# Row-tiled gated heads, loads to spaced partitions, fp32r strips for the last attention, and bias and shared-expert work moved

## The chip, the cores and the metric

The kernel runs on one core of one Trainium2 chip. The metric is device microseconds (us) of one launch, lower is better. The engines are TensorE (PE; its weight loads are shown as PEld), VectorE (DVE), ScalarE (ACT), GpSimd (POOL) and SyncE (SP), which issues most DMAs. They run in parallel and meet at semaphores.

## The reference, cut to what matters

Two batches of 512 tokens with 128 channels go through two decoder layers. Layer 0: layernorm, a gated self-attention (16 heads of 8 channels, scores scaled by a sigmoid gate of the query), mixed with two 4-head attentions ("causal" and "meta"), a one-head cross attention over 77 keys, and a mixture of experts with GELU. Layer 1: layernorm, a self-attention whose inputs are quantised to 8 bits (16 heads of 8), a cross attention with 16 heads of 8 over the 77 keys, and a mixture of experts with SiLU and a shared expert.

```python
scores = einsum('bhqd,bhkd->bhqk', q, k) / sqrt(HD)      # 16 heads, HD = 8
mod    = sigmoid(hidden @ cg_W + cg_b + (cons_vec @ am_W + am_b))
probs  = softmax(scores * mod.transpose(0, 2, 1)[..., None], axis=-1)
ctx    = einsum('bhqk,bhkd->bhqd', probs, v)
```

## The kernel before, in words

**Stages in time.** Start and gated, causal and meta attention (to 305 us of the profiled span), wide cross attention (to 325), `experts_gelu` (to 476), `quantised_attention` (to 640), `cross_attention_heads` (to 738), `experts_silu` (to the end).

**One attention, in steps.** Class `Attention` runs jobs: a job is one group of heads (four gated, two wide) of one batch. `_schedule` writes one list of steps, and each engine walks the same list and does its part:

- A: two score products with queries in the output's rows; DVE takes the negated maximum over the keys (line 487). A job of four heads has 8 A blocks of 2 products (4 query tiles x 2 head pairs).
- M: the maxima are transposed by PE (L424), cast by ACT (L536), split by DVE (L494) and written by SP's DMAs (L560) as further rows of the query stack, so that the next product subtracts the maximum.
- B: the score product again, keys in the output's rows (L438), followed by Exp on ACT (L528). One B is a "unit": one head and one tile of 128 keys, so a job of four heads has 16.
- V: the product of probabilities and values, fp32, four heads in four column strips of 32 (L452). E copies it out (ACT, L542), T transposes it (L461) and DVE divides it.

The list starts with `lead_blocks` A blocks (12 in the gated and the quantised attention) before the first B. In the gated attention it also holds the projections of later heads (P on PE, Q for the second part and the loads), the mixes (C, D), in fixed places counted in units.

**Exactness.** To be as exact as fp32, a query and key are cut into three bf16 parts (or two fp32r parts), and the contraction holds the pairs of parts under each other: 6 pairs x 8 channels = 48 rows, padding to 72 and 2 rows for the maxima (72 rows in A, 74 in B). `sp_load` (L714) issues the loads of such a stack: 6 for a bf16 stack, each from 128 partitions to 8 adjacent partitions times 16 heads. Constant rows (zeros, ones) are spread by three DMAs on ACT's queue at the start.

**Quantised attention.** The bias of the projection enters by 4 fp32 products of one row and 512 columns (L1931) and 8 of 128 (L1935), at the stage's start, ahead of the products with the input. The heads lie in strips of 32 partitions (`StripJob`), bf16.

**Last cross attention.** `PairJob` and `CrossJob` keep two heads in 64-row sides (48 rows used). The queries are loaded by 24 DMAs of 64 KB (two sides x six places x two batches) to 8 partitions each, and a job's maxima by 4 DMAs.

**SiLU experts.** PE first computes the routing logits (L2226, 8 products), then the shared expert's up products for two half batches, waits for the routing on DVE, and goes on through 8 expert pairs.

## Time and profile before

| | us |
|---|---|
| median of 3 runs (797.33 to 806.68) | 806.39 |
| the profiled execution | 810.68 |
| its span, first to last instruction | 808.6 |
| PE / PEld / DVE / ACT / POOL busy | 646.1 / 341.5 / 405.2 / 377.1 / 93.6 |

The profile is one execution of the program. Busy times of engines overlap; what sets the time is read stage by stage, from gaps, from who waits for whom, and from TensorE's granted clock (1.0 is 2.4 GHz, 0.5 is 1.2 GHz), whose mean was 0.801. The difference of 2.1 us between the execution and its span lies around the program.

### The profile page before, as it was taken

How to read it: one execution, taken by the hardware profiler on the slowest of the kernel's cores; microseconds unless marked ns; L12 is line 12 of the kernel's file. 1: busy time of each engine (PE TensorE's matmuls, PEld its weight loads, DVE VectorE, ACT ScalarE, POOL GpSimd, SP SyncE). 2: the span in 40 equal slices, each digit the busy share in tenths (PEclk: the TensorE clock that was granted, in tenths of full speed). 3: DMA queues.
4: the chain of work that ended last, by engine and by line, in shares of the span. 5: the costliest groups of instructions: out<-in, count | busy, mean ns of one | idle time of the engine just before them, and what ended most of it. 6: DMA issues, size and time to landing. Idle time of an engine off the chain costs nothing. (4 is left out here: it accounts for less than half of the span.)

```text
span 808.6 us, 9225 instructions
## 1 busy us (share of the span) xinstructions
PE 646.1 (80%) x3255; PEld 341.5 (42%) x3255; DVE 405.2 (50%) x806; ACT 377.1 (47%) x655; POOL 93.6 (12%) x80
## 2 busy tenths in 40 slices
PE   4089859999996977699999965798888427986798
PEld 2013223333333334599999934112221312324686
DVE  3077546677713755712221346868870723414554
ACT  3026736676663234554444521368885124443321
POOL 4101200110001000700000001980000010002100
PEclk9558989999999577599999965559995655557799
DMA  8405240353005008000000000000000041000000
GB/s 212 83 1 79 29 51 1 50 68 42 3 1 78 2 9 352 0 1 2 13 1 1 1 0 1 0 2 1 2 2 1 0 58 22 2 1 1 0 1 27
DMA packets 15456, 24.28 MB, mean 30 GB/s; under 512 B 2779, under 2 KB 10507, under 8 KB 15027
## 3 DMA queue, kind: packets, MB, share of 16 engines
q1 hardware_dynamic: 14048, 21.77, 14.0%
q10 hardware_dynamic: 1363, 1.93, 1.0%
q8 instruction: 26, 0.43, 0.2%
q14 instruction: 19, 0.16, 0.1%
HBM read 9.99 MB, written 0.52 MB: 13 GB/s over the span
## 5 line engine op out<-in xcount | busy, mean ns | idle before, releaser
L487 DVE TENSOR_REDUCE negmax<-ps 128x2 f32<-128x1024 f32 x96 | 114.5, 1220 | 62.5 <-PE ps L417 62.2
L528 ACT ACTIVATE probs<-ps 128x512 f32<-128x512 f32 x192 | 106.2, 598 | 47.5 <-PE ps L438 45.6
L1604 PEld LDWEIGHTS ps<-wproj,hid 128*128 128x128 f32 x640 | 83.4, 192 | 6.7
L1604 PE MATMUL ps<-wproj,hid 128*128 128x128 f32 x640 | 84.1, 275 | 0.0
L528 ACT ACTIVATE probs_q<-ps,score_scale 128x512 f32<-128x512 f32 x128 | 77.3, 691 | 13.1 <-PE ps L438 12.7
L1654 ACT ACTIVATE hid<-ps 128x512 f32<-128x512 f32 x80 | 47.5, 597 | 66.9 <-PE ps L774 66.9
L774 PE MATMUL ps<-h,wfc 128*128 128x512 f32 x240 | 76.9, 432 | 0.0
L487 DVE TENSOR_REDUCE negmax_q<-ps 128x2 f32<-128x1024 f32 x64 | 73.8, 1209 | 5.6 <-PE ps L417 5.6
L417 PE MATMUL ps<-k_gated,q_gated 72*128 72x512 bf16 x128 | 45.4, 443 | 27.0 <-DMA k_gated<-parts 20.9
L438 PE MATMUL ps<-q_gated,k_gated 74*128 74x512 bf16 x128 | 47.1, 410 | 8.3 <-DMA q_gated<-q_gated 8.2
L1764 DVE SCALAR_TENSOR_TENSOR x_tok<-ps,comb,x_tok 128x128 f32<-128x128 f32 x64 | 18.0, 344 | 69.3 <-PE ps L1604 69.3
L417 PE MATMUL ps<-k_strips,q_strips 32*128 32x512 bf16 x128 | 34.9, 481 | 14.8 <-DVE negmax_q L487 5.9
L438 PE MATMUL ps<-q_strips,k_strips 32*128 32x512 bf16 x128 | 40.2, 467 | 7.8 <-ACT probs_q L528 6.7
L452 PE MATMUL ps<-probs_q,v_q 128*32 128x512 f32 x256 | 44.3, 776 | 0.0
L774 PEld LDWEIGHTS ps<-h,wfc 128*128 128x128 f32 x240 | 41.2, 198 | 4.1
L139 PE MATMUL ps<-ident,xn 128*128 128x128 f32 x48 | 13.8, 440 | 32.4 <-DVE xn L106 32.3
L503 DVE RECIPROCAL inv<-ps 128x16 f32<-128x16 f32 (+1 forms) x32 | 7.7, 240 | 64.0 <-PE ps L461 63.8
L774 PE MATMUL ps<-h_parts,up_parts 128*128 128x512 f32 x108 | 32.7, 444 | 4.2 <-DVE hid L2341 3.2
L452 PE MATMUL ps<-probs,v_gated 128*32 128x512 f32 x256 | 35.5, 628 | 0.0
L452 PE MATMUL ps<-probs,v_wide 128*64 128x512 f32 x128 | 34.5, 628 | 0.3
L417 PEld LDWEIGHTS ps<-k_gated,q_gated 72*128 72x128 bf16 x128 | 10.4, 104 | 54.9 <-issue 27.4
L417 PE MATMUL ps<-k_wide,q_wide 96*128 96x512 f32 x64 | 29.1, 549 | 5.4 <-issue 3.0
(355 smaller groups left out, 919.0 us busy)
## 6 DMA issues: line engine op xcount, KB each, us to landing
q_wide<-parts SPq DMA_DIRECT2D x12, 256.0 KB, 5.5
k_wide<-parts SPq DMA_DIRECT2D x12, 256.0 KB, 6.9
wfc<-in_L_ffn_Wfc_dram SPq DMA_DIRECT2D x1, 2560.0 KB, 9.3
wproj<-in_L_ffn_Wproj_dram SPq DMA_DIRECT2D x1, 2560.0 KB, 15.0
q_gated<-parts SPq DMA_DIRECT2D x12, 128.0 KB
k_gated<-parts SPq DMA_DIRECT2D x12, 128.0 KB
qs_x<-parts_x SPq DMA_DIRECT2D x24, 64.0 KB
w<-in_L_ffn_W_dram SPq DMA_DIRECT2D x1, 1024.0 KB, 17.0
```

Source lines behind the costliest of these rows:

```text
L139: nc.tensor.transpose(K.ps[:, self.banks[b], P * (i % TPB):P * (i % TPB) + P], K.xn[:, i, :], K.ident[:, :]).then_inc(self.turned, 1)
L417: last = nc.tensor.matmul(ps[:, bank, at:at + size], rows, keys, start=True, stop=True, skip_group_check=True)
L438: nc.tensor.matmul(ps[0:size, self.B_BANK + g % self.B_SLOTS, :], job.k_at(j, k0, size, 2), job.q_at(j, job.q0, S, 2), start=True, stop=Tr ...
L452: last = nc.tensor.matmul(ps[job.width * j:job.width * (j + 1), self.O_BANK, :], job.v[0:size, job.b, i, job.heads[j], :], self.probs[0:si ...
L487: nc.vector.tensor_reduce(maxima, scores, AX.X, ALU.max, negate=True).then_inc(self.a_max_done, 1)
L503: nc.vector.reciprocal(inv, tile[:, :, :, hd]).then_inc(self.sums_inverted, 1)
L528: nc.scalar.activation(self.probs[0:size, g % self.P_SLOTS, :], ps[0:size, self.B_BANK + g % self.B_SLOTS, :], ACT.Exp, scale=scale).then_ ...
L774: last = nc.tensor.matmul(out, weights(a), moving(b), start=(start and i == 0), stop=(stop and i == 2), skip_group_check=True)
L1604: last = nc.tensor.matmul(K.ps[:, y_bank(g), i * P:(i + 1) * P], hid[:, m % SLOTS, i * P:(i + 1) * P], wproj[:, FT * e + f, :], start=(f = ...
L1654: nc.scalar.activation(hid[:, m % SLOTS, :], K.ps[:, 2 + m % 4, :], ACT.Gelu).then_inc(n["gelu_done"], 1)
L1764: last = nc.vector.scalar_tensor_tensor(out=K.x_tok[:, t, :], in0=y[:, i, :], scalar=comb[:, t, e:e + 1], in1=K.x_tok[:, t, :], op0=ALU.mu ...
```

## The change

1. **Gated heads.** Two heads share the 128 partitions: each has a side of 64 rows (`PairJob`; 16 slots become 8). The six pairs of parts are written at every 8th partition (`stack[c::8]`: 16 partitions x 8 pairs of heads in one DMA), and the maxima go to rows 6 and 7 of each group of eight. The projection's weights are interleaved by column (`interleaved`), so that heads come out by side. The padding DMAs are gone: DVE fills the whole query stack with zeros, POOL the key stack with ones, and POOL fills rows 96 to 127 of the wide keys. An A block's two products now use the two 64-row halves of the array, and so do neighbouring B's.
2. **Start.** Keys are projected first, after half of the layernorm; three loads of each of the first two stacks are issued by SP, three by ACT (step L). The first job has two heads, and 8 A blocks stand ahead of the first B, growing to 12 over the next 16 units (`lead_growth = 4`).
3. **Quantised attention.** The 4 bias products of 512 columns stand at the end of `experts_gelu`; the 8 of 128 columns become 2 of 512. The same `lead_blocks`, growth and split first job; E moves from ACT to DVE.
4. **Last cross attention.** fp32r in two parts: strips of 32 rows, written at every 4th partition, 3 loads of 256 KB for each batch, one of them by ACT. A is one product of K=128 and 320 columns for a query tile (before: two of K=112 and 154 columns); B has K=32; the maxima of a job go by 2 DMAs.
5. **SiLU experts.** The shared expert's first two up products come ahead of the routing logits, two more before the routing weights are needed.

```diff
 class PairJob(Job):
-    ROWS, SIDE = 48, 64
-    max_dmas = 4
+    SIDE, STEP, PARTS = 64, 8, 6
     def q_at(self, j, t0, n, more):
         at, h = self.SIDE * (j % 2), self.heads[j]
-        return self.q[at:at + self.ROWS + more, h // 2, t0:t0 + n]
+        return self.q[at:at + self.SIDE, h // 2, t0:t0 + n]
...
-class CrossJob(PairJob):
+class CrossJob(Job):
+    stride = CTX_PAD                                    # 80
+    STEP, PARTS = 4, 3
+    def q_at(self, j, t0, n, more):
+        return self.q[32 * j:32 * j + 32, self.heads[0] // 4, t0:t0 + n]
     def products(self, heads, q0):
-        both, first = self.SIDE + self.ROWS, self.heads[0] // 2
-        return [(2 * c * self.keys, 2 * self.keys, self.q[0:both, first + c, q0:q0 + P],
-                 self.k[0:both, first + c, :, self.k0:self.k0 + self.keys]) for c in range(self.G // 2)]
+        g = self.heads[0] // 4
+        return [(0, self.G * CTX_PAD, self.q[:, g, q0:q0 + P], self.k[:, g, :, self.k0:self.k0 + CTX_PAD])]
...
                 wanted = min(len(blocks), (self.held_lead if first else self.lead_blocks)
-                             + 2 * (n // 4) + self.A_PLACES[n % 4])
+                             + 2 * (n // 4) + self.A_PLACES[n % 4] + min(n // 4, self.lead_growth))
...
+            elif kind == "E" and self.evacuate_on_vector:
+                nc.vector.tensor_copy(self.osb[0:rows, u % 2, :], ps[0:rows, self.O_BANK, :])
...
+        if it.get("step"):
+            pairs = PAIRS if it["parts"] == 3 else PASSES
+            places = [(pair[it["kind"] == "k"], it["stack"][c::it["step"], :, it["s0"]:it["s0"] + it["cols"]])
+                      for c, pair in enumerate(pairs)]
...
+def interleaved(nc, out, w, moving, sides):
+    size = P // sides
+    for s in range(sides):
+        last = nc.tensor.matmul(out[s * size:(s + 1) * size], w[:, s::sides], moving, start=True, stop=True,
+                                skip_group_check=True)
+    return last
...
-    q16 = sb("q_gated", [P, 16, T], BF16, st)
-    k16 = sb("k_gated", [P, 16, T], BF16, st)
+    q16 = sb("q_gated", [P, 8, T], BF16, st)
+    k16 = sb("k_gated", [P, 8, T], BF16, st)
...
-            act.wait_ge(filled_pool, 3)
-            act.dma_start(q16[48:72, :, :], zeros.unsqueeze(1).broadcast_to([24, 16, T])).then_inc(padded, 16)
-            act.dma_start(k16[48:74, :, :], ones.unsqueeze(1).broadcast_to([26, 16, T])).then_inc(padded, 16)
-            act.dma_start(wide_k[96:98, :, :], wide_ones.unsqueeze(1).broadcast_to([2, 4, T])) \
-                .then_inc(padded, 16)
...
+            fill_stack(nc.gpsimd, k16[:, :, :], 1).then_inc(made_k, 1)
...
+            nc.gpsimd.memset(wide_k[96:128, :, :], 1.0).then_inc(made_wide, 1)
...
+            fill_stack(nc.vector, q16[:, :, :], 0).then_inc(made_q, 1)
...
+            pe.wait_ge(n["gelu_done"], M)
+            pe.wait_ge(n["constants"], 11)
+            Q.bias_first(K)
             next_ln.turn(pe, 1)
...
+            eng.dma_start(as_f32(X.q[c::4, :, half(b)]), as_f32((q_high, q_low)[part][:, half(b)])) \
+                .then_inc(s["stacked"][b], 16)
...
             for m in range(M + LAG):
-                if m < M:
+                if m == SHARED:
+                    raw()
+                if m < AHEAD:
                     up(m)
-                if m == SHARED:
+                if m == AHEAD - 1:
                     pe.wait_ge(n["made"], 4)
                     pe.wait_ge(n["comb_ready"], 1)
```

How the steps stand on PE at the program's start (names are out<-in; `negmax` is step M, `q_gated,k_gated` with the query named first is a B, with the keys first an A). Before:

```order
L139 MATMUL ps<-ident,xn 128x128 x8
L1203 MATMUL ps<-modulation 128x1
L634 MATMUL ps<-h_ft,square_weights 128x512 x3
L631 MATMUL ps<-square_weights,h_ft 128x128 x4
L417 MATMUL ps<-k_gated,q_gated 128x512 x18
L424 MATMUL ps<-ident,negmax 4x128 x4
L417 MATMUL ps<-k_gated,q_gated 128x512 x6
L438 MATMUL ps<-q_gated,k_gated 128x512
L417 MATMUL ps<-k_gated,q_gated 128x512 x2
```

Of the change:

```order
L796 MATMUL ps<-modulation 64x1 x2
L796 MATMUL ps<-bias_columns,ident 64x19 x2
L796 MATMUL ps<-bias_columns,ident 32x19 x4
L140 MATMUL ps<-ident,xn 128x128 x8
L796 MATMUL ps<-h_ft,square_weights 64x512 x6
L659 MATMUL ps<-square_weights,h_ft 128x128 x4
L438 MATMUL ps<-k_gated,q_gated 128x512 x10
L445 MATMUL ps<-ident,negmax 2x128 x4
L438 MATMUL ps<-k_gated,q_gated 128x512 x6
L459 MATMUL ps<-q_gated,k_gated 128x512
L438 MATMUL ps<-k_gated,q_gated 128x512 x2
```

The first transposition of maxima stands behind 10 A products instead of 18, and the first B behind 16 instead of 24.

On PE where `experts_gelu` ends and `quantised_attention` begins. Before:

```order
L1604 MATMUL ps<-wproj,hid 128x128 x12
L139 MATMUL ps<-ident,xn 128x128 x4
L1574 UNCONDITIONAL_BRANCH
L1927 UNCONDITIONAL_BRANCH
L1931 MATMUL ps<-ones_row,qkv_bias 128x512 x4
L1935 MATMUL ps<-qkv_bias,ones_row 128x128 x8
L1941 MATMUL ps<-xq,wq_high 128x512
```

Of the change:

```order
L1671 MATMUL ps<-wproj,hid 128x128 x12
L1500 MATMUL ps<-ones_row,qkv_bias 128x512 x4
L140 MATMUL ps<-ident,xn 128x128 x4
L1641 UNCONDITIONAL_BRANCH
L2005 UNCONDITIONAL_BRANCH
L2008 MATMUL ps<-qkv_bias,ones_row 128x512 x2
L2015 MATMUL ps<-xq,wq_high 128x512
```

The four wide bias products moved ahead of the last transposition of the layernorm, into the stage before.

SP's DMAs from the quantised to the last cross attention (`mparts` are maxima, L560 or L588). Before:

```order
L560 DMA q_strips<-mparts_q 4x512 x16
L1926 UNCONDITIONAL_BRANCH
L2109 UNCONDITIONAL_BRANCH
L732 DMA qs_x<-parts_x0 8x8x512 x12
L732 DMA qs_x<-parts_x1 8x8x512 x12
L560 DMA qs_x<-mparts_x 1x2x512 x32
```

Of the change:

```order
L588 DMA q_strips<-mparts_q 4x512 x14
L2004 UNCONDITIONAL_BRANCH
L2194 UNCONDITIONAL_BRANCH
L2194 DMA qs_x<-q_high_x 32x4x512
L2194 DMA qs_x<-q_low_x 32x4x512
L2194 DMA qs_x<-q_high_x 32x4x512 x2
L2194 DMA qs_x<-q_low_x 32x4x512
L588 DMA qs_x<-mparts_x 4x512 x16
```

SP issues 5 loads of queries instead of 24 (a sixth is ACT's), and half as many of maxima.

## Rows read from the trace of the kernel before

**Rows 1.** The core's line, and the page's clock row in 40 slices of 20.2 us.

```profile
core 0: 808.6 us, clock 0.801
PEclk9558989999999577599999965559995655557799
```

**Rows 2.** Busy time by stretch, then PEclk, DMA share, GB/s: two load times.

```profile
24.00:38.00 14.00, 0.00 (x0) 0.00 (x0) 0.00 (x0) 0.00 (x0) 1.08 (x1) 0.50 0.55 82
156.00:165.00 9.00, 8.24 (x48) 3.74 (x50) 6.02 (x12) 6.26 (x12) 1.27 (x1) 1.00 1.08 131
```

**Rows 3.** Timeline of the start: start us, us, engine, line, instruction, idle before.

```profile
3.89 3.52 POOL L753 MEMSET v_gated<- 128x4096 f32 x1
10.99 0.58 ACT L128 COPY h_ft<-ps 128x512 f32<-128x512 f32 x1 [2.06 <-PE ps L139]
23.03 5.20 SPq L732 DMA_DIRECT2D k_gated<-parts  x6
23.93 1.15 POOL L709 TENSOR_TENSOR parts<-rest,parts 128x512 bf16<-128x512 f32 x1 [0.79 <-ACT parts L667]
40.35 1.87 PE L417 MATMUL ps<-k_gated,q_gated 72*128 72x512 bf16 x4 [20.89 <-DMA k_gated<-parts]
55.79 0.61 PE L438 MATMUL ps<-q_gated,k_gated 74*128 74x512 bf16 x1
```

**Rows 4.** Timeline: the maxima of the fourth gated job and the B behind them.

```profile
104.33 1.29 SPq L560 DMA_DIRECT2D q_gated<-q_gated  x2
118.29 0.61 PE L438 MATMUL ps<-q_gated,k_gated 74*128 74x512 bf16 x1 [8.15 <-DMA q_gated<-q_gated]
```

**Rows 5.** Busy by stretch (PE PEld DVE ACT POOL, PEclk, DMA): gated and quantised attention.

```profile
56.00:135.00 79.00, 66.54 (x310) 23.63 (x308) 46.20 (x53) 47.81 (x85) 7.16 (x6) 0.85 0.31 41
152.00:217.00 65.00, 61.37 (x334) 23.64 (x332) 46.53 (x56) 45.47 (x84) 5.07 (x4) 1.00 0.37 50
560.00:600.00 40.00, 34.31 (x251) 9.18 (x244) 35.89 (x39) 36.51 (x64) 0.00 (x0) 1.00 0.01 2
118.00:124.00 6.00, 5.71 (x18) 2.11 (x18) 2.45 (x2) 2.41 (x5) 0.00 (x0) 0.50 0.00 0
```

**Rows 6.** Timeline: two A products on one array, 72 rows, and strips of 32.

```profile
49.75 1.03 PE L417 MATMUL ps<-k_gated,q_gated 72*128 72x512 bf16 x2 [0.18 <-DVE negmax L487]
506.24 0.61 PE L417 MATMUL ps<-k_strips,q_strips 32*128 32x512 bf16 x2 [0.53 <-DVE negmax_q L487]
```

**Rows 7.** The reductions of line 487: duration ns min/median/max, first and last start us.

```profile
L487 DVE TENSOR_REDUCE negmax<-ps x96: 1210/1224/1226, 41.4 to 273.9; 128x2 f32<-128x1024 f32 x96
```

**Rows 8.** Timeline around the start of the quantised attention.

```profile
472.20 1.15 PE L139 MATMUL ps<-ident,xn 128*128 128x128 f32 x4 [3.55 <-DVE xn L106]
477.56 7.16 PE L1931 MATMUL ps<-ones_row,qkv_bias 1*128 1x512 f32 x8 [4.21 <-PEq L57]
484.52 3.62 PE L1935 MATMUL ps<-qkv_bias,ones_row 1*128 1x128 f32 x16
503.18 1.03 PE L417 MATMUL ps<-k_strips,q_strips 32*128 32x512 bf16 x4 [3.83 <-DVE q_strips L1923]
515.54 1.18 SPq L560 DMA_DIRECT2D q_strips<-mparts_q  x2
517.89 0.60 PE L438 MATMUL ps<-q_strips,k_strips 32*128 32x512 bf16 x1 [0.59 <-DMA q_strips<-mparts_q]
```

**Rows 9.** Timeline: the last cross attention's loads, first A and first B.

```profile
649.70 15.70 SPq L732 DMA_DIRECT2D qs_x<-parts_x  x24
663.81 1.21 PE L417 MATMUL ps<-ks_x,qs_x 112*128 112x154 bf16 x8 [13.79 <-DMA qs_x<-parts_x]
675.53 0.64 PE L438 MATMUL ps<-qs_x,ks_x 50*77 50x512 bf16 x1 [4.62 <-DMA qs_x<-mparts_x]
```

**Rows 10.** Timeline: SiLU experts, the routing weights ready and the next up product.

```profile
758.47 0.29 DVE L2363 TENSOR_TENSOR comb_parts<-comb_rest,comb_parts 128x128 bf16<-128x128 f32 x1
763.84 1.65 PE L774 MATMUL ps<-h_parts,up_parts 128*128 128x512 f32 x6 [0.93 <-ACT comb_t L2297]
```

More of the change, by code:

```diff
@@ L712, in threes, with loads, load @@
         return self.number(n, lambda x: x["kind"] in "qk" and x["parts"] == 3)
-    def sp_load(self, sp, n):
+    def loads(self, n):
+        it = self.items[n]
+        if it.get("step"):
+            pairs = PAIRS if it["parts"] == 3 else PASSES
+            places = [(pair[it["kind"] == "k"], it["stack"][c::it["step"], :, it["s0"]:it["s0"] + it["cols"]])
+                      for c, pair in enumerate(pairs)]
+            return sorted(places, key=lambda x: x[0])
+        places, row, hd, count = [], 0, it["hd"], it["parts"]
+        for size in range(count, 0, -1):
+            for part in range(size):
+                at = row + hd * (part if it["kind"] == "q" else size - 1 - part)
+                places.append((part, it["stack"][at:at + hd, :, it["s0"]:it["s0"] + it["cols"]]))
+            row += size * hd
+        return sorted(places, key=lambda x: x[0])
+    def load(self, eng, n, first=0, end=None):
         it = self.items[n]
@@ L1454, in __init__ @@
         self.v = sb("v_x", [P, NB, 1, 16, 32])
         self.full = sb("full_kx", [P, keys])
-        self.rest = sb("rest_kx", [P, keys])
-        self.parts = sb("parts_kx", [P, 3, keys], BF16)
-        self.n = {x: K.sem("kx_" + x) for x in ("made", "projected", "full", "first", "rest", "second", "third", "v_out",
-                                                "stacked")}
-        self.item = dict(kind="k", stack=self.k, hd=8, parts=3, s0=0, cols=keys, pair=True)
-    MADE = 6
+        self.parts = sb("parts_kx", [P, 2, keys], F32R)
@@ L1464, in constants, with bias @@
+        self.n = {x: K.sem("kx_" + x) for x in ("made", "projected", "full", "first", "second", "v_out", "stacked")}
+    def bias(self, name):
+        at = COLUMNS.index(name)
+        return self.K.by_strip[:, at:at + 1]
+    MADE = 8
     def constants(self, pool):
         ops, chain = self.K.nc.gpsimd, Chain(pool, self.n["made"])
-        chain(ops.memset(self.k[:, :, :, :].rearrange("p c s t -> p (c s t)").bitcast(F32), 0.0))
-        chain(ops.memset(self.k[32:64, :, 0, :], 1.0))
-        chain(ops.memset(self.k[96:128, :, 1, :], 1.0))
+        keys = as_f32(self.k[:, :, :, :])
+        chain(ops.memset(keys.rearrange("p g j t -> p (g j t)"), 0.0))
+        for j in range(4):
+            chain(ops.memset(keys[32 * j:32 * j + 32, :, j, :], 1.0))
@@ L1514, in load @@
         n, loads = self.n, 0
-        sp.wait_ge(n["made"], 3)
-        for part in range(3):
-            sp.wait_ge((n["first"], n["second"], n["third"])[part], 1)
-            row = 0
-            for size in range(3, 0, -1):
-                if part < size:
-                    for dst, rows in stack_places(self.item, row + 8 * (size - 1 - part)):
-                        sp.dma_start(dst, self.parts[rows, part, :]).then_inc(n["stacked"], 16)
-                        loads += 1
-                row += size * 8
+        sp.wait_ge(n["made"], 5)
+        for c, (_, part) in enumerate(PASSES):
+            sp.wait_ge(n[("first", "second")[part]], 1)
+            for j in range(4):
+                for b in range(NB):
+                    sp.dma_start(as_f32(self.k[32 * j + c:32 * j + 32:4, :, j, b * CTX_PAD:b * CTX_PAD + CTX_LEN]),
+                                 as_f32(self.parts[32 * j:32 * j + 32, part, b * CTX_LEN:(b + 1) * CTX_LEN])) \
+                        .then_inc(n["stacked"], 16)
+                    loads += 1
         sp.wait_ge(n["stacked"], 16 * loads)
@@ L2134, in _ @@
             ln.vector(dve)
-            stks[0].split(dve, nc.vector)
+            for b in range(NB):
+                low_part(dve, b)
             att.vector(dve)
@@ L2364, in _ @@
                                     ALU.subtract).then_inc(n["comb_ready"], 1)
-            for m in range(SHARED):
-                product(m)
             cut_low(dve, 2)
```

377 lines of the change are left out of this document (219 added, 158 removed).

## The prediction

> **What bounds the kernel now.** I read the clock first: TensorE was granted 0.801 on average, 0.5 from 20 to 60 us, high in both gated stages, low again in the last cross attention [rows 1]. Then the timeline of the start. The first score product begins at 40.35 after a wait of 20.89 us for the loads of the key stack, the first B at 55.79, and in between PE does 24 A products at half clock while each A block waits for DVE [rows 3]. So 40 us pass before anything repeats, half of it for DMAs; those run at a DMA share of only 0.55 and 82 GB/s, where loads of the wide stacks to more partitions reach 1.08 and 131 GB/s [rows 2].
>
> Then busy times by stretch [rows 5]. In the gated stage of batch 0 (79 us for 64 units) and batch 1 (65 us, again 64) DVE has 46.2 and 46.5 us of work and ACT 47.8 and 45.5, but PE 66.5 and 61.4: PE is the bound there. Batch 0 holds one stall as well, 8.15 us for the maxima of the fourth job: SP issues them at 104.33, and B starts at 118.29 [rows 4]; they lie in the queue behind stack loads. In the quantised stage, the same work with heads in strips of 32 rows, DVE and ACT are busy for 35.9 and 36.5 of 40 us and PE is not the bound. Why PE is slower in the gated stage is in the timeline: two A products of 72 rows take 1.03 us one behind the other, while two of 32 rows, side by side in the array, take 0.61 [rows 6], both while the clock was 0.5. The reductions take 1.22 us each in both stages [rows 7].
>
> **The change part by part.** The sum is made against the profiled execution's own 810.7 us; the median of the runs shown, 806.4, is 4.3 below.
>
> 1. *Start, first A.* The new loads go to 16 partitions instead of 8, and the padding DMAs are gone (24 and 26 rows x 16 heads x 1024 tokens x 2 bytes: 1.6 MB). No row shows such a destination. From below: they gain nothing and stay at 82 GB/s (131 KB in 1.6 us, six in 9.6 us). From above: 131 GB/s or better (1.0 us each). I take the upper, as the copied size is that of the wide loads' class and the padding no longer competes. The chain that feeds them is earlier too: the projections need only half of the layernorm, ready on ACT at 10.99 + 0.58 = 11.6 [rows 3], but POOL, which makes the parts, first fills stacks (3.52 us for 4096 words, rows 3; three such fills, some 12 us) and is free at about 15. Before, POOL's last part ended at 25.1 and A started 15.3 behind. Now the last parts are there at about 21, SP and ACT issue in parallel, and six loads at 1.0 us land by 27: first A at **27, −13.4**. At 82 GB/s it would be 31. DVE's fill of the query stack at the very start costs about 3.5 us, hidden under the loads of x but for 0.5.
>
> 2. *Fill, first A to first B.* 15.4 us for 24 products and a round trip of maxima. Now 16 products stand ahead of B, and the maxima start behind 10. Eight products fewer are four blocks of 1.22 us [rows 7] = 4.9, of which 0.5 is lost to the round trip showing: **−4.4**.
>
> 3. *Gated, batch 0.* If pairs of products on two 64-row halves overlap as strips do [rows 6], PE's work falls by 0.4 us in each A block and about as much for B pairs, to about 45 us, and DVE and ACT become the bound. The batch costs the busier one's time over the share that it reaches in the quantised stage (36.5 of 40, so 0.90): DVE 46.2 plus the four postponed blocks 4.9 = 51.1, over 0.90 = 57. The clock stays low for the first part, as it was from 40 to 66; there PE needs up to 0.3 us more a unit for some 24 units: +7. 79 − 64.5 = **−14.5**. The stall of 8.15 lies in the 79, and its cause (a queue of slow loads) goes with part 1.
>
> 4. *Gated, batch 1.* 46.5/0.90 = 52: **−13**. The two causal stages start with fewer leftovers: −1.5.
>
> 5. *Quantised attention.* The bias products take 7.16 and 3.62 us at half clock [rows 8]. The first four move ahead of the layernorm's last transposition, where PE stood idle for 3.55 us [rows 8]; at full clock they take 3.6 and fit. If they don't hide, they cost up to 3.6 there. The 8 small ones (3.62) become 2 wide ones (half of 7.16): nothing. So −7.2. The fill from first A (503.18) to first B (517.89) shrinks like part 2, −4.2, of which DVE gives back 2.5 later where it is near its limit. A split first job has another M, E and T: +1. E moves from ACT, 0.6 us a job, to DVE: between −3 and +3, taken 0. Sum **−7.9**.
>
> 6. *GELU experts.* POOL's fills and the key loads of the last attention lie in a stage of 150 us in which POOL has little to do: 0. If they slow SP's weight loads, +2.
>
> 7. *Last cross attention.* SP's 24 loads of 64 KB take 15.70 us and PE waits 13.79 for them [rows 9]; now there are six of 256 KB to 32 spaced partitions, of which ACT issues one. At 131 GB/s [rows 2] six take 12 us but they start as each half is ready; the first batch's three, 6 us, release the first job: first A at 655.5 instead of 663.8, **−8.3**. The fill to the first B (11.7 us, B waits 4.62 for maxima) loses two of four DMAs a job, −2.5. In the steady part B strips overlap but fp32r A products of 320 columns cost more: −3 (from 0 to −6). Sum **−13.8**.
>
> 8. *SiLU.* The routing, which ended at 758.47, starts two up products later, and one more is done by then (six take 1.65 or 2.93 us): +0.5, from −1 to +4 [rows 10].
>
> Sum: −13.4 −4.4 −14.5 −13 −1.5 −7.9 −13.8 +0.5 = −68.0, so 743 for a profiled execution and 739 unprofiled; I say 740.
>
> On the loads, by the Trainium skill ("SBUF — State Buffer", section "Door 1: The DMA port swizzle") eight adjacent partitions reach two of the 16 ports, 16 partitions spaced by 8 reach eight, and 32 spaced by 4 all sixteen. By that rule the cross attention's loads would be twice as fast as I took, and its first A 3 us earlier; the low share of rows 2 agrees with it, and no row shows a spaced destination.
>
> **The rivals.**
>
> *Pairs don't overlap.* Only strips of 32 have been seen side by side. If 64-row halves run one behind the other, gated PE time stays at 61 a batch: batch 1 gains nothing and batch 0 only its stall and part of the fill, so 20 of the 27.5 go: 763. For it: no row shows two 64-row halves at work. Against: rows 6. Chance 0.15.
>
> *Low clock persists.* PE's busy share falls in the gated stage, and the clock was 0.5 in stretches where PE waits a lot (20 to 60, and 650 to 730, rows 1), as well as in 118 to 124, where PE was busy for 5.71 of 6 us [rows 5]. At half clock a unit costs 1.2 us (five Exps in 6 us) instead of 0.9. For half of the 128 units: +20, 763. Chance 0.12.
>
> *Loads stay slow.* First A at 31 or later, the stall of rows 4 comes back (8), the cross attention's 8 are lost: 4 + 8 + 8 + 8 for further waits: about 769. Chance 0.08.
>
> *Upside.* The last cross attention is all at half clock [rows 1]. If denser work brings it to full clock it is 15 to 20 us shorter: 722. Chance 0.08.
>
> *Slower than before.* B of 64-row halves and V in column strips alternate at each unit, with M and T as whole-array products between. If each change of split lets the array drain for about a product's time, 0.61 [rows 6], 130 changes cost 78 and the 27.5 of parts 3 and 4 are lost: 848. It makes the kernel 2% slower from (826.6 − 743 − 27.5)/130 = 0.43 us a change. Against it: the quantised stage alternates in the same way, 40 us for some 54 units. Chance 0.03.
>
> The Trainium skill ("TensorEngine Tiling (Array Packing)", section "Key Properties") says that changing the tiling mode, not just the tile, drains the engine; by it the gated stages would lose something at each change; what it costs with strips is small enough for DVE and ACT to reach their share in [rows 5].
>
> **How the numbers follow.** The forecast, 740, has 0.54; its own range is ±13 from the ends above (start 4, clock term 7, quantised 4, cross 6, SiLU 3, most not together). The others: 0.15 at 763, 0.12 at 763, 0.08 at 769, 0.08 at 722, 0.03 at 848. From 716 to 768 leaves out the drain, half of the slow loads and the forecast's tails: 2 in 10. 2% is about what a measurement of this kernel tells from no change: 790 to 823. Below lie all but the drain and mixtures of two or three bad cases: faster 0.93, same 0.04, slower 0.03.
>
> **What would show it.** Start: the first score product near 27, with a DMA share near 1 from 18 to 27. Gated: pairs of A products in 0.6 us at low clock, DVE and ACT at 0.9 of the stretch, no idle for maxima at the fourth job; 64 units in 57 to 65 and in 52 us. Quantised: no row of one-row products behind the layernorm but two; first B 10 to 11 us after the first A. Cross: the first A within 15 us of the stage's start, a wait for maxima under 3. Wrong would make it a mean clock below 0.75, a pair that takes 1.0 us, or a new wait of DVE, which holds E in the quantised stage, seen in B's releasers as the maxima's split.

## The result, and the profile after

The changed kernel took 775.81 us (median of 4 runs, 767.06 to 776.76); its ratio to the kernel before, run beside it, is 0.963 with a 95% interval of 0.951 to 0.975. A second series gave 771.07 us and 0.955 (0.951 to 0.960). It is faster, by 31 us in the first series where 66 were forecast (806.4 to 740). The profiled execution has a span of 775.0 us (808.6 before).

```profile
core 0: 775.0 us, clock 0.830
PEclk9669999999995756799999966689995655557899
```

The line above and the page's clock row (40 slices of 19.4 us) answer to [rows 1]: the start's low stretch is shorter, the gated stages run at a mean clock of 0.93 (42 to 112, low only at its start) and 1.00 (129 to 194), and the last cross attention (629 to 697) is at half clock as before.

The start, from the timeline (start us, us, engine, line, instruction, idle before):

```profile
9.28 1.78 DVE L104 RECIPROCAL std<-std 128x4 f32<-128x4 f32 x1
11.11 4.25 DVE L107 TENSOR_SCALAR xn<-x_tok,mv,std 128x128 f32<-128x128 f32 x4
11.45 3.51 POOL L1251 MEMSET k_wide<- 32x4096 f32 x1
15.92 5.36 PE L796 MATMUL ps<-h_ft,square_weights 128*64 128x512 f32 x12
19.37 1.95 SPq L774 DMA_DIRECT2D k_gated<-parts  x3
31.67 1.04 PE L438 MATMUL ps<-k_gated,q_gated 64*128 64x512 bf16 x4 [9.30 <-DMA q_gated<-parts]
41.70 0.61 PE L459 MATMUL ps<-q_gated,k_gated 64*128 64x512 bf16 x1 [0.49 <-DMA q_gated<-mparts_gated]
```

The first A comes at 31.67 (40.35 before, [rows 3]), the first B at 41.70 (55.79). The first projection starts at 15.92, although half of the input was normalised at 11.1; DVE's second half takes 4.25 us beside POOL's fill of the wide keys.

Busy time by stretch (PE, PEld, DVE, ACT, POOL, then clock, DMA share, GB/s), the 64 units of batch 0 and of batch 1 of the gated attention; the third row is the loads' wait at the start:

```profile
42.30:112.10 69.80, 63.11 (x331) 17.64 (x328) 50.70 (x60) 48.12 (x87) 7.16 (x6) 0.93 0.25 47
129.40:194.20 64.80, 59.90 (x332) 19.33 (x333) 46.06 (x55) 45.11 (x83) 5.10 (x4) 1.00 0.38 50
27.00:31.60 4.60, 0.00 (x0) 0.00 (x0) 0.00 (x0) 0.00 (x0) 0.66 (x1) 0.50 0.64 171
```

Batch 0 takes 69.8 us (78.5 before) and batch 1 64.8 (65.0 before). In batch 1 DVE and ACT have the work of [rows 5] (46.1 and 45.1 us; DVE is busy for 0.71 of the time), and PE is nearly as busy as before (59.9, 61.4 before), though two A products in a pair now take 0.39 us and did take 0.60 at this clock. The new loads move 171 GB/s, against 82 in [rows 2].

Where the time went, from the starts of the first and last instruction of each part in the two timelines (us):

| part | before | after | moved | forecast |
|---|---|---|---|---|
| to the first A | 40.4 | 31.7 | -8.7 | -13.4 |
| first A to first B | 15.4 | 10.0 | -5.4 | -4.4 |
| gated batch 0, 64 units | 78.4 | 69.7 | -8.7 | -14.5 |
| gated batch 1, 64 units | 65.0 | 64.8 | -0.2 | -13 |
| the causal attentions | 39.8 | 40.3 | +0.5 | -1.5 |
| meta attention to GELU's last down products | 226.2 | 228.5 | +2.3 | 0 |
| quantised attention, from there to its last eight units | 151.5 | 146.8 | -4.7 | -7.9 |
| to the last cross attention's 24th unit | 95.2 | 83.6 | -11.6 | -13.8 |
| SiLU, with the end of the cross attention | 96.1 | 98.9 | +2.8 | +0.5 |

To see inside the gated stages, the starts of ACT's Exp instructions were taken every four units (a cycle: four B, two A, one V):

```
cycles of batch 1, us      8 with projections and mixes                2 with A of their own    6 with A of the causal heads
before                     5.0 5.4 3.8 4.3 3.6 5.4 4.0 4.0 (35.5)      3.0 4.4 (7.4)            3.1 4.1 3.3 4.4 3.1 4.1 (22.1)
after                      4.6 5.4 3.8 4.3 3.5 5.4 4.2 4.0 (35.2)      2.6 4.1 (6.7)            3.3 4.2 3.5 4.5 3.3 4.2 (23.0)
```

Only the two cycles in the middle behave as forecast. Two such cycles of after, on PE and DVE; first with A of the gated heads' own, then with the causal heads' (K of 96 rows, fp32r, the whole array):

```profile
163.27 1.06 PE L473 MATMUL ps<-probs,v_gated 128*32 128x512 f32 x8
164.27 0.39 PE L459 MATMUL ps<-q_gated,k_gated 64*128 64x512 bf16 x1
164.28 0.59 PE L438 MATMUL ps<-k_gated,q_gated 64*128 64x512 bf16 x2
164.50 0.58 PE L459 MATMUL ps<-q_gated,k_gated 64*128 64x512 bf16 x2
165.66 1.06 PE L473 MATMUL ps<-probs,v_gated 128*32 128x512 f32 x8
...
173.19 1.07 PE L473 MATMUL ps<-probs,v_gated 128*32 128x512 f32 x8
174.19 0.39 PE L459 MATMUL ps<-q_gated,k_gated 64*128 64x512 bf16 x1
174.50 0.73 PE L438 MATMUL ps<-k_wide,q_wide 96*128 96x512 f32 x2
175.17 0.39 PE L459 MATMUL ps<-q_gated,k_gated 64*128 64x512 bf16 x2
175.49 0.73 PE L438 MATMUL ps<-k_wide,q_wide 96*128 96x512 f32 x2
176.15 0.39 PE L459 MATMUL ps<-q_gated,k_gated 64*128 64x512 bf16 x1
176.47 1.07 PE L473 MATMUL ps<-probs,v_gated 128*32 128x512 f32 x8
```

From V to V the first takes 2.39 us (two reductions of 1.2 on DVE, which is never idle there), the second 3.28, PE without a gap. In the first, A starts 0.01 us after B, since one of its two products lies on the other half; in the second, every step from a half to the whole array or back shows 0.31 to 0.32 us from a single product's start to the next start.

### The profile page after: what moved, and what is told of

It reads as the page before. It is cut to its first block and busy times, and to the rows that moved or that the text cites. A ratio compares the mean times of both kernels' runs of the same rounds, so it can differ in the third digit from the quotient of the medians.

```text
span 775.0 us, 9266 instructions
## 1 busy us (share of the span) xinstructions
PE 638.4 (82%) x3271; PEld 329.1 (42%) x3271; DVE 419.2 (54%) x824; ACT 374.7 (48%) x649; POOL 97.2 (13%) x78
## 3 DMA queue, kind: packets, MB, share of 16 engines
q1 hardware_dynamic: 12436, 20.78, 11.7%
## 5 line engine op out<-in xcount | busy, mean ns | idle before, releaser
L473 PE MATMUL ps<-probs_q,v_q 128*32 128x512 f32 x256 | 46.8, 730 | 0.0
L438 PE MATMUL ps<-k_gated,q_gated 64*128 64x512 bf16 x128 | 29.8, 427 | 20.1 <-DMA q_gated<-parts 9.3
L459 PE MATMUL ps<-q_strips,k_strips 32*128 32x512 bf16 x128 | 38.5, 438 | 5.7 <-ACT probs_q L556 4.0
L438 PE MATMUL ps<-k_strips,q_strips 32*128 32x512 bf16 x128 | 31.6, 442 | 12.4 <-DVE negmax_q L509 4.4
L459 PE MATMUL ps<-q_gated,k_gated 64*128 64x512 bf16 x128 | 39.5, 394 | 1.3 <-ACT probs L556 0.8
L473 PE MATMUL ps<-probs,v_gated 128*32 128x512 f32 x256 | 39.1, 612 | 0.0
L731 POOL TENSOR_TENSOR parts<-full,parts 128x512 fp32r<-128x512 f32 x8 | 10.2, 1272 | 159.5 <-ACT parts L688 159.5
L438 PE MATMUL ps<-k_wide,q_wide 96*128 96x512 f32 x64 | 26.4, 505 | 4.5 <-issue 2.8
```

The costliest lines, as they stand in the source:

```text
L438: last = nc.tensor.matmul(ps[:, bank, at:at + size], rows, keys, start=True, stop=True, skip_group_check=True)
L459: nc.tensor.matmul(ps[0:size, self.B_BANK + g % self.B_SLOTS, :], job.k_at(j, k0, size, 2), job.q_at(j, job.q0, S, 2), start=True, stop=Tr ...
L473: last = nc.tensor.matmul(ps[job.width * j:job.width * (j + 1), self.O_BANK, :], job.v[0:size, job.b, i, job.heads[j], :], self.probs[0:si ...
L731: ops.tensor_tensor(self._part(n, 1), full, as_f32(self._part(n, 0)), ALU.subtract) \
```

## Experiments

Each is the changed kernel with one edit, unless said otherwise. Times of stages are from each run's own profile, so that they don't depend on how the kernel before fared beside it (its medians were 798 to 809 in the four series). "Batch 1" is its 64 gated units; they take 64.8 us in all eight profiles whose edits leave its cycles alone, so that 0.7 us there is clear.

The quantised stage, counted from its first Exp to that of the last cross attention, took 149 us in both profiles of the changed kernel and 142 to 150 in variants that leave it as it is. The long ones spent more of it at a clock of 0.5: 64 us of 149.3 in the changed kernel (with four dips of 3.4 us and more between 500 and 568), 43 of 142.3 in the variant that changes only the last stage. So totals of 768 to 776 are told apart only by their stages.

### What a change of the array's split costs

A kernel of its own: x is copied, and TensorE does series of products on zeros, with no waits.

```diff
+cycle(b, a): b(0); a(); b(1); b(2); a(); b(3); v()     # v: four fp32 products in four column strips
+cycle(b, a), grouped: b(0); b(1); a(); a(); b(2); b(3); v()
```

> This kernel computes nothing of the reference: it only copies x and lets TensorE do series of products of 512 columns on zeros, with no wait between them: whole-array bf16; 64-row halves in turn; one half alone; whole and half in turn; and ten cycles each of the order B A B B A B V (V: four fp32 products in four column strips) with B of 74 rows or of 64-row halves, A of two 96-row fp32r products or of two bf16 products. Drain theory (a change of the array's split costs about 0.1 us, read from 0.32 us between starts after a change against 0.21 without): whole and half in turn 0.31 us a product at full clock against 0.21; the cycle with fp32r A takes 2.95 us with 74-row B and 3.2 to 3.3 with 64-row B; the cycle with bf16 A takes 2.7 with 72 and 74 rows and 2.3 to 2.4 with halves. No-drain theory: whole and half in turn 0.21; the cycle with fp32r A gets 0.2 us shorter with halves, 2.75. Grouped order B B A A B B V: drain theory 2.9 or less with fp32r A, no-drain theory 2.5.

Measured, timeline of PE at full clock:

```profile
27.57 7.07 PE L79 MATMUL ps<-mov_whole 128*128 128x512 bf16 x31
34.57 3.63 PE L79 MATMUL ps<-mov_halves 64*128 64x512 bf16 x32
38.04 7.07 PE L79 MATMUL ps<-mov_one_half 64*128 64x512 bf16 x32
45.36 10.00 PE L79 MATMUL ps<-mov_mixed 64*128 64x512 bf16 x31 [0.26 <-issue]
```

Per product, of 32 each: whole array 0.22 us, halves in turn 0.11, one half alone 0.22, whole and half in turn 0.31. So a change costs 0.09. What in the array takes that time isn't told apart. The cycles, V to V, each the same within 0.02 us in ten repeats:

| cycle | B of 74 rows (before) | B of 64-row halves (after) | grouped, halves |
|---|---|---|---|
| A of two fp32r products, 96 rows | 2.92 | 3.28 | 2.77 |
| A of the gated heads' own | 2.84 | 1.97 | 1.97 |

The drain theory holds for the first row (2.95 and 3.2 to 3.3 were expected). The kernel's own cycle with wide A stands exactly at 3.28, so PE bounds it. In this series the change makes it 0.36 us longer; in the kernel the six cycles with wide A went from 22.1 to 23.0, 0.15 each, as they weren't at PE's 2.92 before. For the second row the theory's sizes were off (2.7, and 2.3 to 2.4, were expected), but the row says why the own cycles gain: PE's 2.84 fell under DVE's 2.44.

### What the overlap is worth in place

```diff
+            self.a_blocks = [([qt], [[j], [j + 2]]) for j in range(2) for qt in range(TPB)]
+            self.units = [(kt, j) for kt in range(TPB) for j in (0, 1, 3, 2)]
```

> Only the order of heads within a gated job is changed: an A block's two products, and neighbouring B's, lie on the same 64-row side, so they can't overlap, while loads, splits and everything else stay. If overlap is worth what the rows show (a pair takes 0.39 instead of 0.60 at full clock, 0.61 instead of 1.03 at half), and PE is what binds: batch 1's 64 units, 64.8 us now, take 20 A blocks and 16 B pairs x 0.21 = 7.6 us more, 72; batch 0's 69.7 us about 8 to 12 more; total about +16 us, 792. If the chain of waits (DVE, ACT's evacuation of projections) binds: less than +4 us in each batch, total under +8.

Measured 777.3 us (the profiled execution 770.84); batch 0 70.6, batch 1 66.6 (+1.8), causal attention of batch 0 +1.7. The edit takes away only part of the overlap. Within an A block and between two neighbouring B's it is gone, but a B and the A next to it now often lie on different sides and start together:

```profile
167.00 0.39 PE L466 MATMUL ps<-q_gated,k_gated 64*128 64x512 bf16 x1
167.00 0.60 PE L445 MATMUL ps<-k_gated,q_gated 64*128 64x512 bf16 x2
```

In batch 1 two such products start within 0.1 us of each other 36 times in the changed kernel and 15 times here. The 21 lost overlaps are worth 4.4 us at 0.21 each; PE's busy time rose by 3.6 us (59.9 to 63.5), and the batch by 1.8. So the view that PE alone binds falls, since half of what PE lost did not show. What batch 1 would take without any overlap, no run says. That gain and cost are a draw is read from the cycles themselves: -0.7 in the two with A of their own, +0.9 in the six with wide A, -0.3 in the eight with projections and mixes.

### Another order of A and B

```diff
 class GatedAttention(Attention):
+    A_PLACES = (0, 0, 2, 2)
```

> Only the places of A in the gated attention's list are changed: B B A A B B V instead of B A B B A B V, so a cycle of four units has two B pairs instead of one and two changes of split fewer where A is a wide whole-array product. Drain theory: where A is wide (some 24 units of each batch) 3.28 us a cycle becomes about 2.9; where A is gated, B pairs save up to 0.21 a cycle; with 0 to 0.3 of waiting for DVE at the second A; the two batches together 3 to 6 us shorter, total about 771. Waits theory: two A's in a row find no free slot, DVE is starved between, and each cycle gets longer by 0.3 to 1.0 us: total +5 to +15.

Measured 800.73 us, batch 1 80.2. PE alone needs less in this order (2.77), but the stage is 1 us a cycle slower, so the waits theory holds for it. Timeline, last column the wait:

```profile
206.63 0.60 PE L445 MATMUL ps<-ident,negmax 128*2 128x128 f32 x4 [1.67 <-DVE negmax L509]
209.88 0.61 PE L459 MATMUL ps<-q_gated,k_gated 64*128 64x512 bf16 x2
210.42 1.73 PE L438 MATMUL ps<-k_wide,q_wide 96*128 96x512 f32 x4
211.68 1.23 DVE L509 TENSOR_REDUCE negmax<-ps 128x2 f32<-128x1024 f32 x1 [2.63 <-PE ps L438]
```

PE waits 1.67 us for the maxima of the group it has just done, and while it does M, T and V, DVE has nothing to reduce for 2.63.

The same in the last cross attention alone, where PE is never idle:

```diff
+class CrossAttention(Attention):
+    A_PLACES = (0, 0, 2, 2)
```

> Only in the last cross attention A goes to the order B B A A B B. There PE is never idle in the steady part (7.43 us a job at half clock), DVE needs 0.8 us an A, so a second B pair that overlaps saves 0.64 us for each of eight jobs: 39.3 us from the first Exp to the 25th becomes 36 to 36.8, total -4 to -5 us. Rival, from the grouped gated list that got 1 us a cycle slower: the second A waits for DVE, 0.3 us or more a job comes on top and the gain is under 2 us.

Measured 775.14 us; the stretch of 24 units went from 39.3 to 40.9 us. PE now waits for DVE at M and for the Exp behind it; the rival holds here too.

### What binds the cycles with a projection

```diff
-            last = interleaved(nc, K.ps[:, bank, 0:it["cols"]], it["w"], ...)
+            cols = it["cols"] if n < 4 else 64
+            last = interleaved(nc, K.ps[:, bank, 0:cols], it["w"], ...)
```

> Left out: seven eighths of the columns of every query, key and gate projection inside the gated attention's list (64 columns instead of 512 are computed; ACT, DVE, POOL and the loads do all their work, on old data). PE then needs 0.9 us less for each of them: 3 of batch 1's gated part in the list's first half of batch 0, and 4 in batch 1. If PE's own time for projections is what keeps batch 1 at 1.01 us a unit: 64.8 becomes about 61. If ACT's two reads of 0.68 us (the wait of 0.8 us of A for them) bind instead: 63.5 to 65.

Batch 1 62.9 us: -1.9 of the 3.6 that PE was spared. Neither of the two.

```diff
-        nc.scalar.activation(full, product, ACT.Identity, bias=it["bias"])
+        c = cols if n < 4 else 64
+        nc.scalar.activation(full[:, 0:c], product[:, 0:c], ACT.Identity, bias=it["bias"])
```

> Left out: seven eighths of ACT's first read of each wide projection's result inside the gated attention's list (`full`, 64 columns instead of 512; the rest of it is old data), 0.45 us of the 1.37 that ACT needs before A gets the slot. PE, DVE, POOL and loads do all their work. If the chain PE projection, ACT's reads, A, DVE's reduction sets the cycles with a projection: 0.3 to 0.45 us less for each of the four in batch 1's gated part, its 64.8 us becomes 63.0 to 63.6. If these cycles are bound by the sum of PE's work: no change, 64.6 to 64.9.

Batch 1 64.1 us: -0.7, of 1.8 spared on ACT. Both edits together:

> Left out: seven eighths of the columns of PE's projections inside the gated attention's list and of ACT's first read of them, as in the two kernels that left out one of them. One chain: the savings add up or more, batch 1's gated part 62.2 us or less (64.8 - 1.9 - 0.7), 61 if what the first removes lets the second show in full. Two things side by side, of which each hides the other: 62.5 to 63.

61.8 us, -3.0. Each of the three is one execution. The savings add up, and in the same cycles (the second, sixth and seventh get 0.4 to 0.5 us shorter by the first edit, 0.2 to 0.4 by the second, 0.7 to 0.8 by both), as one chain would have it: P holds one of the two slots for PE's 1.1 us and ACT's 1.4, and A and DVE have the other. Of the 5.4 us spared, 2.4 still don't show. The waits of after in batch 1 (PE, what it waited for: us, times, longest) name the same step:

```profile
PE ps L438 <- ACT parts L688: 2.4, 3, 0.8
PE ps L438 <- DVE v_wide L705: 0.8, 2, 0.4
```

A direct try, a bank of its own for everything but A, taken from B:

```diff
 class GatedAttention(Attention):
+    B_SLOTS, OWN_BANK = 2, 6
```

> In the gated attention the results of projections, transpositions and mixes (P, M, T, C, D) get a PSUM bank of their own instead of one of the two slots that A blocks use; in return B has two banks instead of three. Everything else stays. Slot theory (in cycles of four units with a projection, A waits since a slot is held for 1.1 us by PE and 1.4 us by ACT's two reads, so DVE is served by one slot): those cycles, 4.6 to 5.4 us, fall by 0.5 to 1.0 us each, batch 1's 64.8 us becomes 57 to 61, both batches together about 10 us less. Sum-of-work theory (in these cycles PE or ACT simply have too much to do): no cycle falls by over 0.2 us. Should two B banks be too few, PE shows waits on ACT at B and the cycles without projection, 2.6 to 3.5 us, get longer; that would be seen apart.

Measured 783.8 us, batch 1 69.5: PE waits 5.8 us on ACT's Exp at B (8 times, longest 1.1). Two banks for B are too few, and the cycles with a projection got longer, not shorter. What a slot more would bring stays open; no bank is left to try it with.

### Lead, and E on DVE

```diff
-        super().__init__(K, "att0", jobs, lead, 8, ...)                       # lead_growth = 4
+        super().__init__(K, "att0", jobs, lead, 12, ...)                      # lead_growth = 0
-    att = QuantAttention(K, "attq", jobs, 2, 8, ...)
+    att = Attention(K, "attq", jobs, 2, 12, ...)                              # first job of four heads
```

> The gated and the quantised list start with 12 A blocks and don't grow, as in the kernel before, and the quantised attention's first job has four heads again; all else stays. Theory that the shorter lead is only a loan: gated, first B 4 to 5 us later (46.5 instead of 41.7) and batch 0's 64 units 4 to 5 us shorter (65), so the causal attention starts at the same time within 1 us; quantised, first B 4.7 us later after the first A, the first 32 units 4 us shorter, the stage the same within 1 us. Theory that it gains in full: the first B later by 4.7 and no unit faster, total +8 to +9 us.

Measured 774.31 us (768.39 in the profiled execution, the fastest of five). Gated: the first Exp comes at 46.7 instead of 42.3, and the 64th is over at 112.1 in both. The shorter lead is a loan, paid back in full within batch 0. Quantised: the first Exp comes 3.0 us later, and the stage takes 137.8 us after it, where the shortest variants with the short lead take 142.2 to 142.3: 1.5 in favour of the long lead, in profiles whose clock isn't the same (49 us at 0.5 against 43), so this one is less sure. The split first job went out with the short lead, and no run parts the two.

```diff
-    att = QuantAttention(K, "attq", jobs, 2, 8, ..., evacuate_on_vector=True)
+    att = QuantAttention(K, "attq", jobs, 2, 8, ...)
```

> Only step E of the quantised attention (0.67 us for each job) goes back from DVE to ACT. DVE theory (DVE binds at full clock, two reductions of 1.22 in a cycle of 2.5): each of the nine jobs' cycle with E and T gets 0.3 to 0.6 us shorter, the stage about 3 to 5 us, total 771 to 773. Rival, ACT binds (four Exp of 0.61 to 0.69 in the same 2.5): the stage gets 0 to 4 us longer.

Measured 769.08 us. Four cycles (a job) with E on DVE take 2.5 4.6 2.6 2.5 (12.2), with E on ACT 2.8 3.8 2.6 2.5 (11.7), as before. So DVE binds, and moving E to it costs 0.5 us a job, 4 us in all by that. The whole stage is 142.3 us, as short as that of a variant with E on DVE that had 10 us less at the clock of 0.5, so its length alone doesn't show it. The combination further on does: with a lead of 12 its first 120 units take 89.3 us with E on ACT, where the variant above, with E on DVE, takes 93.5 (10 and 15 us of them at 0.5).

### The two ends of the program

```diff
-                if m == SHARED:
-                    raw()
+            raw()                                          # the whole stage as before
```

> Only the last stage goes back to the order of before: routing logits first, then the shared expert. If the new order costs what the two profiles say (96.1 us from the last attention's end to the end of the program before, 98.9 after, the wait of 4.9 us for the routing weights among it), this gets 2.8 us shorter; if the 2.8 comes from the clock there, no change.

Measured 767.78 us (767.73 to 769.47); from the last attention's 24th unit to the end 96.4 us instead of 98.9. The new order costs 2.5. Its wait, in the changed kernel, answers to [rows 10]:

```profile
728.13 1.04 PE L2366 MATMUL ps<-ident_bf,comb_parts 128*72 128x128 bf16 x8 [4.86 <-DVE comb_parts L2468]
```

```diff
-            ln.tensor(pe)
+            ln.turn(pe, 0)                      # and in P of the values: ln.turn(pe, 1) ahead of it
-            for b in range(NB):
-                ln.normalise(dve, b)
-            dve.wait_ge(gate_ready, 3)
+            ln.normalise(dve, 0)
+            dve.wait_ge(gate_ready, 3)          # then the gate's bias, then ln.normalise(dve, 1)
```

> At the start PE transposes only the first half of the normalised input ahead of the projections of batch 0, and the second half behind the query's projection; DVE sums the gate's bias ahead of normalising the second half. In the changed kernel the first projection starts at 15.92 since PE and DVE do the second half first, whose normalisation takes 4.25 us while POOL fills the wide keys (1.11 in the kernel before). If the projection's start is what sets the first A: first projection at 12.3, first A at 28 instead of 31.7, total -3.5. If POOL (busy with fills to 14.96) or the loads set it: first A not before 30.5.

Measured 769.63 us, first Exp at 37.1. Timeline:

```profile
10.44 1.31 DVE L107 TENSOR_SCALAR xn<-x_tok,mv,std 128x128 f32<-128x128 f32 x4
11.19 4.80 PE L796 MATMUL ps<-h_ft,square_weights 128*64 128x512 f32 x12 [0.67 <-ACT h_ft L129]
26.41 1.03 PE L438 MATMUL ps<-k_gated,q_gated 64*128 64x512 bf16 x4 [8.93 <-DMA q_gated<-parts]
```

The first projection starts 4.7 us earlier, and the first A comes at 26.41, 5.3 earlier and where the prediction had it (27). The projection's start was the missing step.

### A kernel that beats both, and the changed one again

The early projection, the last stage's order of before, E on ACT and a lead of 12 in the quantised attention, all in one:

> The changed kernel with what the runs found: early projection at the start (-5.2 us to the first Exp), the quantised attention with E on ACT (-0.5 us a job), 12 A blocks of lead and a four-head first job (first Exp 3 to 4.7 us later, 4.5 us less after it), and the last stage in the order of before (-2.5). Sum against the changed kernel: -5.2 - 4 - 0.5 - 2.5, about -12; if the quantised stage gets its full clock as in the variants so far (767 to 769 us where the changed kernel shows 767 or 776), 755 to 760; if these gains only shift the clock, 764 or more.

> The changed kernel itself once more. If the 7 us by which its profiled quantised stage is longer than that of variants which don't touch it come from the clock of an execution: its times fall into two groups, about 767 to 769 and 775 to 777, and no variant needs a gain of its own for 768. If they are its own work: all times at 775 or more.

Measured side by side: 758.13 us (755.21 to 760.70), ratio to the kernel before 0.940 (0.935 to 0.944), and the changed kernel 771.07 (768.62 to 774.55), ratio 0.955 (0.951 to 0.960). The combination is 13 us faster than the changed kernel, of which the quantised stage has the most: 131.6 us from its first Exp where the changed kernel shows 149, though its longer lead makes that first Exp some 4 us later. The changed kernel's times (five of six between 770.75 and 774.55) lie between the two groups that were expected, so they don't sort into two; its profile again has 149.1 us in that stage and the dips of the clock, which the combination's lacks. Why the clock dips in one and not in the other stays open: two variants that differ from the changed kernel only in a later stage (the grouped cross attention and the last stage's old order) don't dip.

## Why the prediction was wrong, step by step

**Gated batch 1, -13 forecast, -0.2 measured: this is the step that failed.** The prediction took the whole batch at the quantised stage's busy share, DVE's 46.5 us over 0.90, since both have "the same work". Measured, DVE is busy for 46.1 us of 64.8, a share of 0.71. The two stages don't have the same work. In the quantised list there are only A, B, V and their rounds; in batch 1 eight of sixteen cycles carry projections and mixes, and six carry the A blocks of the causal heads. Both could be read before: the fixed places of P, Q, C and D in the list, and a lead of 12 blocks, that is 24 units. Three sizes were wrong in it:

- The saving of a pair was read at half clock (1.03 to 0.61, [rows 6]) and applied to a stage at full clock, where it is 0.60 to 0.39. It was half as large.
- The changes of split were priced as a rival only, at a whole product's 0.6 us, and dismissed, as the quantised stage alternates freely. It does so among 32-row products and column strips only for V; in the gated stage each A of the causal heads takes the whole array between two B's. The price is 0.09 us in the plain series, and 0.36 in a cycle of the series after the overlap's gain is taken off, of which 0.15 shows in the kernel. The rival's mechanism is there; its threshold of 0.43 us a change is not reached. The rule of the Trainium skill that it named ("TensorEngine Tiling (Array Packing)", "Key Properties") agrees with the series of whole and half in turn (0.31 us a product against 0.22).
- In the cycles with a projection, much of what PE is spared turns into waiting for the slot: 3.0 us come back when the projections and ACT's reads are cut short. Batch 1 is then still 10 us above the forecast's 52. As an estimate, at the quantised stage's 12.2 us for four cycles the eight with projections and mixes would take 24.4 instead of 35.2, and the six with wide A some 18 instead of 23.0. So the excess lies in the two kinds that the quantised list doesn't have; beyond the 3.0 its cause stays open.

No rival fits. "Loads stay slow" is nearest in time (769), and had the first A "at 31 or later", where it came (31.67), by luck: the loads were fast and began late. "Pairs don't overlap" (763) has batch 1 unchanged, as it was, and is false in its mechanism: they do overlap. Its premise, that only strips of 32 had been seen side by side, was false too. The kernel before had it in its last cross attention, two B's of 50 rows at rows 0 and 64 in the time of one:

```profile
687.69 0.65 PE L438 MATMUL ps<-qs_x,ks_x 50*77 50x512 bf16 x2
```

**Gated batch 0, -14.5 forecast, -8.7 measured.** The stall of [rows 4] went, as forecast: its cycle takes 4.2 us instead of 12.3, and that is 8.1 of the 8.7. Against it stands the loan of the short lead (4.3), so some 4.9 us are left. They are not the overlap's: with the lead of before (the variant above), batch 0 takes 65.4 us, 13.0 less than before, and beside the 8.1 of the stall 4.7 of these lie in four cycles during which the kernel before ran in part at a clock of 0.5 (56 to 66, 87 to 90, 114 to 124). The changed kernel was at 0.5 only up to 52. The forecast had kept 7 us for the low clock (its 57 and 7 make 64, not 64.5). That the clock makes these 4.7 is read from the coincidence and not isolated; the other cycles are the same draw as in batch 1.

**Start, -13.4 forecast, -8.7 measured.** The loads were right: 171 GB/s, better than the 131 taken as a bound (at a DMA share of 0.64, where near 1 was to show it). The last parts were ready at 27.7 instead of 21. The forecast had the projections follow half of the layernorm; in the code PE transposes all eight tiles first, and DVE's second half was held up by POOL's fills, which had been costed at nothing for DVE. The early projection gives the missing 5 us. **The fill, -4.4**, was -5.4.

**Quantised attention, -7.9 forecast, -4.7 measured.** Up to the first A the gain was 6.2 of the 7.2: the four bias products did not hide wholly, they take 4.48 us and the layernorm's last transposition starts 7.2 us after GELU's last products instead of 6.4. The fill gave 4.7. Behind the first Exp, 120 units took 105.0 us instead of 98.7: E on DVE, taken as 0 between -3 and +3, costs 4, and the short lead is paid back there too, 4.5 by the variant with the long one, of which the forecast had 2.5. That makes more than the 6.3; the clock, at 0.5 for 30 us of these and for 41 before, may hide the difference.

```profile
448.43 4.48 PE L1500 MATMUL ps<-ones_row,qkv_bias 1*128 1x512 f32 x8
458.16 3.75 PE L2008 MATMUL ps<-qkv_bias,ones_row 1*128 1x512 f32 x4 [4.20 <-PEq L58]
476.83 1.03 PE L438 MATMUL ps<-k_strips,q_strips 32*128 32x512 bf16 x4 [3.82 <-DVE q_strips L2001]
486.82 0.60 PE L459 MATMUL ps<-q_strips,k_strips 32*128 32x512 bf16 x1 [0.40 <-DMA q_strips<-mparts_q]
```

These answer to [rows 8].

**Last cross attention, -13.8 forecast, -11.6 measured.** The loads and the fill brought more than forecast: PE waits 3.02 us where it waited 13.79 ([rows 9]), and the time to the first Exp fell by 14.7 in all. The prediction took 131 GB/s for these loads and thought twice as much possible; the six moved 360 (625.7 to 630.0). The steady part, forecast at -3, is +3.0 for 24 units: a job takes 7.43 us instead of 6.84.

```profile
628.53 1.31 PE L438 MATMUL ps<-ks_x,qs_x 128*128 128x320 f32 x4 [3.02 <-DMA qs_x<-q_low_x]
656.16 0.90 PE L438 MATMUL ps<-ks_x,qs_x 128*128 128x320 f32 x2
657.00 0.71 PE L459 MATMUL ps<-qs_x,ks_x 32*77 32x512 f32 x2
```

An A block of 320 columns takes 0.84 us to the next start where it took 0.62, two per job, and each B 0.06 more; the B pair overlapped before too. Its overlap had been counted as new.

**SiLU, +0.5 forecast, +2.8 measured,** 2.5 of it the new order. **Between, 0 forecast, +2.3:** the wide cross attention ran at a mean clock of 0.58 in 22 us (281 to 303) where it was 0.72 before (303 to 325); that this makes the 2.3 is not shown.

## What to carry to other kernels

A stage that is bound by one engine in one stretch is bound by others a few microseconds on: cut it into cycles, sort these by what they carry, and cost each kind, before a share from another stage is laid over the whole. Read a pair's saving at the clock of the stage that it is meant for, and count the products of another shape that lie between. Of three work moves in this change (E, the expert's order, the short lead) one was a loan and two cost time, while the gain lay in loads and in a stall that went.

## What the runs showed of the hardware

- Two products on the two 64-row halves take 0.11 us each in a series, where one half alone takes 0.22, as the whole array does; a change between the whole array and a half adds 0.09 us, at full clock.
- Loads to more partitions, spaced, are fast: 171 GB/s at a DMA share of 0.64 to 16 partitions, every 8th, against 82 GB/s at 0.55 to eight adjacent ones ([rows 2]). The six loads of 256 KB to 32 partitions, every 4th, moved 360 GB/s at 0.97 (window, us, busy times, clock, share, GB/s). How much is the spacing's and how much the number of partitions' or the size's, no run tells apart.

```profile
625.70:630.00 4.30, 1.31 (x4) 0.91 (x4) 1.41 (x2) 2.07 (x3) 0.00 (x0) 0.85 0.97 360
```

- DVE's normalising `TENSOR_SCALAR` waits for POOL's fills. In the changed kernel one begun at 9.02 ended at 11.05, one begun at 11.37 at 15.04, each 0.1 us after a fill of POOL (10.97, the wide values; 14.96, the wide keys), and the four tiles took 4.25 us instead of 1.11. The reciprocal begun at 9.28 ended at 11.05 too, behind the first of them. It is not all of DVE's work: the statistics of x took 0.27 us each under POOL's fill of the gated values, and in the kernel before a reciprocal took its usual 0.18 in the middle of a fill:

```profile
7.84 1.81 POOL L753 MEMSET v_wide<- 128x2048 f32 x1
8.78 0.18 DVE L103 RECIPROCAL std<-std 128x4 f32<-128x4 f32 x1 [1.71 <-ACT std L122]
```

The Trainium skill ("SBUF — State Buffer", section "Who interferes with whom") says that the two engines share a port pair, which DVE takes only in some of its instructions, `tensor_scalar` among them, and that whoever has it first holds it for a whole instruction. The trace agrees: the blocked ones end within 0.1 us of POOL's, and the others are not blocked.
